# Conv 2's difference plane in three rounded passes in a fused residual block of two 3x3 convolutions

## The reference

```python
def _conv3x3(x, w): ...                     # NCHW, stride 1, padding 1
def _bn(x, gamma, beta, mean, var):
    inv = gamma * rsqrt(var + EPS)
    return x * inv[None, :, None, None] + (beta - mean * inv)[None, :, None, None]
identity = x
out = relu(_bn(_conv3x3(x, w1), g1, b1, m1, v1))
out = _bn(_conv3x3(out, w2), g2, b2, m2, v2)
return relu(out + identity)
```

## Time and profile before

| | |
|---|---|
| median of 3 runs | 596.51 us (595.66 to 597.7) |
| the profiled execution | 596.25 us |
| its span, first to last instruction | 594.3 us |
| PE busy | 576.5 us, 97% of the span |
| PEld busy | 533.7 us, 90% |
| DVE busy | 555.3 us, 93% |
| ACT busy | 472.6 us, 80% |
| mean granted TensorE clock | 0.994 |

### The profile page before, as it was taken

One profiled execution on the slowest core, in us unless ns is written; L12 is line 12 of the kernel. 1 busy time (PEld: TensorE's weight loads), 2 busy tenths in 40 slices (PEclk: granted clock), 3 DMA queues, 4 the chain that ended last, 5 costly groups with the idle time before them and its releaser, 6 DMA issues.

```text
span 594.3 us, 8667 instructions
## 1 busy us (share of the span) xinstructions
PE 576.5 (97%) x2962; PEld 533.7 (90%) x2962; DVE 555.3 (93%) x475; ACT 472.6 (80%) x730; POOL 19.8 (3%) x28
## 2 busy tenths in 40 slices
PE   6769999999999999999999999999999999999997
PEld 3769999999999999999999999999999999999996
DVE  6899999999999999999999999999999999999963
ACT  5687888887788887788887778888778888778874
POOL 7500000000000000000000000000000000000000
PEclk9799999999999999999999999999999999999999
DMA  4112223322223331232332222332122233121012
GB/s 161 56 61 88 104 84 110 112 82 82 83 83 110 110 108 56 83 109 84 110 110 67 89 92 83 110 110 93 71 83 93 100 110 110 58 82 51 29 55 108
DMA packets 22458, 53.23 MB, mean 90 GB/s; under 512 B 1584, under 2 KB 18096, under 8 KB 22448
## 3 DMA queue, kind: packets, MB, share of 16 engines
q1 hardware_dynamic: 22304, 52.80, 25.0%
q10 hardware_dynamic: 144, 0.29, 0.2%
HBM read 27.40 MB, written 25.69 MB: 89 GB/s over the span
## 4 chain that ended last, share of the span: by engine, by line
PE 93%; DVE 2%; ACT 1%; issue 0%; POOL 0%
PE psum L639 93%; DVE x_outer L367 1%; DVE x_lo L375 1%; DVE psum L389 1%; ACT w_mat L488 0%; DVE t_outer L412 0%; POOL g_t L181 0%; ACT psum L514 0%; DVE t_inner L398 0%; DVE x_inner L355 0%; ACT out_sb L563 0%; ACT z L534 0%; ACT z L535 0%; DVE x_inner L359 0%
## 5 line engine op out<-in xcount | busy, mean ns | idle before, releaser
L639 PE MATMUL psum<-x_hi,w_hi 128*128 128x392 f32 (+2 forms) x512 | 175.3, 342 | 6.7 <-DVE x_lo L375 6.7
L639 PE MATMUL psum<-x_hi,w_lo 128*128 128x392 f32 (+2 forms) x512 | 175.8, 343 | 0.0
L639 PE MATMUL psum<-x_lo,w_hi 128*128 128x392 f32 (+2 forms) x512 | 175.1, 342 | 0.0
L389 DVE TENSOR_TENSOR psum<-psum,z 128x784 f32<-128x784 f32 (+1 forms) x128 | 127.1, 993 | 21.3 <-ACT hidden L540 9.9
L639 PEld LDWEIGHTS psum<-x_hi,w_hi 128*128 128x128 f32 x512 | 97.0, 189 | 8.3 <-issue 4.8
L639 PEld LDWEIGHTS psum<-x_hi,w_lo 128*128 128x128 f32 x512 | 97.0, 189 | 0.4
L639 PE MATMUL psum<-t_inner,w_mat 128*128 128x392 f32 x256 | 94.7, 492 | 2.7 <-ACT psum L514 2.7
L639 PEld LDWEIGHTS psum<-x_lo,w_hi 128*128 128x128 f32 x512 | 97.0, 189 | 0.4
L563 ACT ACTIVATE out_sb<-psum 128x784 f32<-128x784 f32 x64 | 52.8, 825 | 47.1 <-PE psum L639 47.0
L639 PE MATMUL psum<-h_lo,w_hi 128*128 128x392 f32 x256 | 87.3, 341 | 0.0
L639 PE MATMUL psum<-h_hi,w_hi 128*128 128x392 f32 x256 | 87.2, 341 | 0.0
(11 more groups left out here) (67 smaller groups left out, 747.5 us busy)
## 6 DMA issues: line engine op xcount, KB each, us to landing
x_sb<-x_dram SPq DMA_DIRECT2D x32, 814.0 KB, 4.3
out_dram<-out_sb SPq DMA_DIRECT2D x64, 392.0 KB, 2.8
w_raw<-w_dram ACTq DMA_DIRECT2D x1, 288.0 KB, 3.5
w_raw<-w_dram SPq DMA_DIRECT2D x1, 288.0 KB, 5.4
bn<-params_dram SPq DMA_DIRECT2D x1, 132.0 KB, 3.7
```

Source lines behind the costliest of these rows:

```text
L389: nc.vector.tensor_tensor(psum[:, half, EVEN:ODD + 1, 0:width], t1, z[:, half, :, 0:width], ALU.add).then_inc(joined[conv], 1)
L639: ins = nc.tensor.matmul(psum[:, half, bank, first:first + (j1 - j0) * WQ], w[:, i, far, :], moving, start=not onto and at == 0, stop=at = ...
```

## The change

- T2 of conv 2 is treated as T1 is: `high_hidden("inner")` on ACT and `split_hidden("inner")` on DVE take both inner planes of `t_inner` in one instruction each (`ti_hi`, `ti_lo`), and its product is three rounded passes.
- The semaphore that releases ACT's rounding is now raised by `difference_hidden`, not by `sum_hidden`. PE waits for `hlo_ready["inner"]` ahead of both inner products. `sum_hidden` no longer waits for PE, since PE no longer reads `t_inner`.
- `x_inner` and `x_outer` have rows of 29 instead of 28 columns; `outer_x` subtracts one run of 812 elements a plane.
- `x_hi` and `x_lo` lose their zero edge rows, and POOL the eight memsets; conv 1's products skip the edge in their indices.
- `w_raw`, `g_t` and `g_sum` lie in the tiles `z` (conv 1) and `out_sb` (conv 2).
- The loop covers steps 2 to 25; 26 to 33 are written out. The first load of image 1 is written ahead of the steps.
- In the tail's step N both inner planes are split together, half by half.

The core of the diff:

```diff
+    RUN = NQ * (WQ + 1)
-        x_outer = sb("x_outer", [P, 2, NQ, WQ])
-        x_inner = sb("x_inner", [P, TBUFS, 2, NQ, WQ])
+        x_outer = sb("x_outer", [P, 2, RUN])
+        x_inner = sb("x_inner", [P, TBUFS, 2, RUN])
-        t1_hi = sb("t1_hi", [P, NP, WQ], F32R)
-        t1_lo = sb("t1_lo", [P, NP, WQ], F32R)
+        ti_hi = sb("ti_hi", [P, 2, NP, WQ], F32R)
+        ti_lo = sb("ti_lo", [P, 2, NP, WQ], F32R)
+        spare = {1: z[:].rearrange("p h s r -> p (h s r)"), 2: out_sb[:].rearrange("p h s r -> p (h s r)")}
-            with eng.Fori(0, (N - 4) // 4) as turn:
+            with eng.Fori(0, (N - 8) // 4) as turn:
-            for s in range(N - 2, N + 2):
+            for s in range(N - 6, N + 2):
-            if which == "t1":
-                return t_inner[:, 0, rows], t1_hi[:, rows], t1_lo[:, rows]
+            if which == "inner":
+                return t_inner[:, :, rows], ti_hi[:, :, rows], ti_lo[:, :, rows]
-            for t in (x_hi, x_lo):
-                for b in range(2):
-                    for row in (0, NQ + 1):
-                        nc.gpsimd.memset(t[:, b, :, row, :].bitcast(F32), 0.0).then_inc(zeroed, 1)
...
-                nc.vector.tensor_tensor(x_outer[:], cells[:, :, :, 0:WQ], cells[:, :, :, 1:WQ + 1],
+                nc.vector.tensor_tensor(x_outer[:], runs(cells, 0, XPLANE), runs(cells, 1, XPLANE),
                                         ALU.subtract).then_inc(tx_ready["outer"], 1)
...
-                wait(dve, inner[2], 4 * n)
+                wait(dve, hlo_ready["inner"], n)
                 nc.vector.tensor_tensor(t_inner[:, 0, rows], hid_data[:, 0, rows, 0:WQ], hid_data[:, 1, rows, 0:WQ],
-                                        ALU.add).then_inc(th_ready["t1"], 1)
+                                        ALU.add)
...
-                                        ALU.subtract).then_inc(th_ready["t2"], 1)
+                                        ALU.subtract).then_inc(th_ready["inner"], 1)
...
                 if last:
-                    split_hidden("t1", s - 1, kl % 2)
+                    split_hidden("inner", s - 1, kl % 2)
...
                 if last:
-                    high_hidden("t1", s - 1, kl % 2)
+                    high_hidden("inner", s - 1, kl % 2)
...
-                if (conv, i) == (2, 2):
-                    return ((t_inner[:, 1], wmat[2]),)
-                elif i == 1:
-                    hi, lo = t1_hi, t1_lo
+                elif i in (1, 2):
+                    hi, lo = ti_hi[:, i - 1], ti_lo[:, i - 1]
...
-                pe.wait_ge(th_ready["t2"], n + 1 + more)
+                pe.wait_ge(hlo_ready["inner"], n + 1 + more)
                 pe.wait_ge(res_ready, 2 * n + half + 1)
                 sum_products(2, half, 2, SUM_T2, passes_of(2, 2, 0), True).then_inc(inner[2], 1)
-
-                pe.wait_ge(hlo_ready["t1"], n + 1 + more)
                 sum_products(2, half, 1, SUM_T1, passes_of(2, 1, 0), True).then_inc(inner[2], 1)
```

More of the change, by code:

```diff
@@ L31, in residual_block @@
     WQ = W // 2
-    assert P == 128 and N % 4 == 0
+    assert P == 128 and N % 4 == 0 and N > 8
     HALF1 = ((0, (NP + 1) // 2), ((NP + 1) // 2, NP))
@@ L65, in residual_block, with scratch @@
         out_sb = sb("out_sb", [P, 2, 2, (NQ // 2) * WQ])
-        w_raw = {1: sb("w1_raw", [P, 3, 3, C]), 2: sb("w2_raw", [P, 3, 3, C])}
+        spare = {1: z[:].rearrange("p h s r -> p (h s r)"), 2: out_sb[:].rearrange("p h s r -> p (h s r)")}
+        def scratch(conv, at, kinds):
+            size = kinds * 3 * C
+            return spare[conv][:, at:at + size].rearrange("p (k h c) -> p k h c", k=kinds, h=3)
+        w_raw = {conv: scratch(conv, 0, 3) for conv in (1, 2)}
         bn = sb("bn", [P, 8 + 4 * C])
@@ L75, in residual_block @@
         bias = sb("bias", [P, 2])
-        g_t = {1: sb("g1_t", [P, 4, 3, C]), 2: sb("g2_t", [P, 4, 3, C])}
-        g_sum = {1: sb("g1_sum", [P, 3, C]), 2: sb("g2_sum", [P, 3, C])}
+        g_t = {conv: scratch(conv, 9 * C, 4) for conv in (1, 2)}
+        g_sum = {conv: scratch(conv, 21 * C, 1)[:, 0] for conv in (1, 2)}
         wmat = {1: sb("w1_mat", [P, 4, 2, P]), 2: sb("w2_mat", [P, 4, 2, P])}
@@ L111, in residual_block @@
         xlo_ready = {"inner": sem("xlo_inner"), "outer": sem("xlo_outer")}
-        th_ready = {"t1": sem("th_t1"), "t2": sem("th_t2"), "outer": sem("th_outer")}
-        hhi_ready = {"t1": sem("hhi_t1"), "outer": sem("hhi_outer")}
-        hlo_ready = {"t1": sem("hlo_t1"), "outer": sem("hlo_outer")}
+        th_ready = {"inner": sem("th_inner"), "outer": sem("th_outer")}
+        hhi_ready = {"inner": sem("hhi_inner"), "outer": sem("hhi_outer")}
+        hlo_ready = {"inner": sem("hlo_inner"), "outer": sem("hlo_outer")}
         inner = {1: sem("inner1"), 2: sem("inner2")}
@@ L230, in newton_step, with runs, until @@
             after(eng.tensor_tensor(inv[:, part], inv[:, part], tmp[:, part], ALU.mult))
[L232 to L238, removed]
+        def runs(cells, first, step):
+            return cells[:, first:first + 2 * step].rearrange("p (s r) -> p s r", s=2)[:, :, 0:RUN]
         def x_full(which, k):
             full, places = (x_outer[:], slice(0, 2)) if which == "outer" else (x_inner[:, k], slice(2, 4))
-            return full.rearrange("p s j q -> p s (j q)"), places
+            return full.rearrange("p s (j c) -> p s j c", c=WQ + 1)[:, :, :, 0:WQ], places
         def x_part(t, k, places):
-            return t[:, k % 2, places, 1:NQ + 1, :].rearrange("p s j q -> p s (j q)")
+            return t[:, k % 2, places]
+        def until(n, k):
+            return (n - k % 2) * 8 + 16
         def hidden_rows(half):
@@ L277, in _ @@
             load(sp, 0, 0)
[L278 removed]
+            sp.dma_start(w_raw[2], w2).then_inc(w_in[2], 16)
+            load(sp, 1, 1)
             def step(s, k):
[L281 removed]
+                if not isinstance(s, int) or 0 <= s < N - 2:
                     wait(sp, tx_ready["outer"], s + 3 - XBUFS)
@@ L513, in residual @@
                 for i, bank, share in ((0, SUM_T1, 0.5), (1, SUM_T2, -0.5)):
-                    ins = nc.scalar.activation(psum[:, half, bank, 0:width],
-                                               x_inner[:, k, i, j0:j1, :].rearrange("p j q -> p (j q)"),
-                                               ACT.Copy, scale=share)
+                    ins = nc.scalar.activation(psum[:, half, bank, 0:width].rearrange("p (j q) -> p j q", q=WQ),
+                                               x_full("inner", k)[0][:, i, j0:j1], ACT.Copy, scale=share)
                 ins.then_inc(res_ready, 1)
@@ L522, in high_hidden @@
                 act.wait_ge(th_ready[which], n + 1 + (half or 0))
-                wait(act, *((inner[2], 4 * n) if which == "t1" else (outer[2], 2 * (n - 1))))
+                wait(act, *((inner[2], 4 * n) if which == "inner" else (outer[2], 2 * (n - 1))))
                 nc.scalar.activation(hi, full, ACT.Copy).then_inc(hhi_ready[which], 1)
@@ L571, in step @@
                     residual(N - 1, kl, 0)
-                    high_hidden("t1", N - 1, kl % 2, 0)
+                    high_hidden("inner", N - 1, kl % 2, 0)
                     relu_hidden(N - 1, 1)
@@ L576, in step @@
                     copy_sum(2, N - 1, 0)
-                    high_hidden("t1", N - 1, kl % 2, 1)
+                    high_hidden("inner", N - 1, kl % 2, 1)
                     residual(N - 1, kl, 1)
```

35 lines of the change are left out of this document (21 added, 14 removed).

## The result

The changed kernel takes 639.25 us, median of 4 runs (637.29 to 640.38), against 596.09 us (595.57 to 597.7) for the kernel before: ratio 1.0716, interval 1.0681 to 1.075. The forecast was 639.7 us, 631 to 648.

The account below looks back on a forecast made before the run. PE's list bound the kernel at 17.62 us a period; a closed round of waits would replace it at 19.06. 29 x (19.06 - 17.62) = 41.8, + 1.2 + 0.5 = 43.5 on 596.25: 639.7 us, range 631 to 648.

Parts of the forecast that it names:

- J: DVE's join that begins a period; the walk starts from it at 0 and reaches the next one at 19.06 us.
- HH: ACT's rounding of the inner planes; waits for difference_hidden, starts at 2.92 us, grows from 0.89 to 1.55 us.
- RO: ACT's relu_out, queued behind the rounding; starts at 4.38 us and ends at 5.21.
- K: DVE's join that waits for relu_out; starts at 5.34 us instead of 4.48, DVE standing still for 0.86 us.
- TI: DVE's split of both inner planes; starts at 7.17 us, ends at 9.01, lengthened by 0.85 us.
- E: PE's first inner product of a period; its first matmul waits for the whole split and starts at 9.07 us.
- the detour over RO: DVE's join waits for relu_out, queued behind ACT's rounding: 0.86 us a period; without it the round is 18.20 us.
- A: Rival: PE keeps the bound and its 15.4 us saving is kept, 580.9 us; chance 0.05.
- B: Rival: the waits hide and DVE's list alone decides, 17.90 us a period, 606.0 us; chance 0.03.
- C: Rival: only the split's length counts, relu_out coming early enough, 18.20 us a period, 614.8 us; chance 0.04.
- rival D: The main case with TensorE's clock falling in each pause, 2.85 us lost each time, 723 us; chance 0.03.
- The end: Last full step +0.57 us, tail's two inner products save 0.48, 0.4 given back for its split waits: +0.5 us.

Follow-up runs that it names:

- RO ahead of the rounding: The changed kernel with ScalarE's relu_out of conv 2's half 0 put ahead of the rounding of the two inner planes: 614.81 us.
- the split ahead of sum_x as well: The changed kernel with relu_out ahead of the rounding and, on VectorE, the split of the two inner planes ahead of sum_x: 601.66 us.
- half the split: The changed kernel with VectorE splitting only the sum plane; the difference plane's third pass reads the sum plane's low part: 613.45 us.
- three passes for half 1 only: The kernel before with the difference plane in three rounded passes for half 1 of the rows, relu_out ahead of the rounding: 588.96 us.
- three passes for half 0 only: The kernel before with three rounded passes for half 0 and the plain product for half 1, halves exchanged against the mixed kernel: 608.78 us.
- the first two experiments: The changed kernel with relu_out ahead of the rounding, 614.81 us; then with the split ahead of sum_x as well, 601.66 us.

## Why the prediction was right

**The bound and its replacement** held. The walk had, from J at 0: HH at 2.92, RO at 4.38, K at 5.34, TI at 7.17, E at 9.07, next J at 19.06. The rows of after give 303.52 - 300.60 = 2.92, 4.39, 5.30, 7.13, 9.03 and 19.04. The experiments then priced the terms one by one. The means over the 29 periods from J of step 2 to J of step 31 are:

| kernel | J of step 2, us | J of step 31, us | mean period, us |
|---|---|---|---|
| before | 49.41 | 560.37 | 17.62 |
| after | 53.30 | 604.68 | 19.01 |
| RO ahead of the rounding | 51.72 | 579.41 | 18.20 |
| the split ahead of sum_x as well | 51.16 | 566.61 | 17.77 |
| the three passes undone | 52.48 | 617.98 | 19.50 |
| half the split | 49.41 | 576.70 | 18.18 |
| three passes for half 1 only | 48.47 | 552.22 | 17.37 |
| three passes for half 0 only | 49.63 | 572.93 | 18.04 |

So the detour over RO costs 0.81 us a period (walked: 0.86), TI's added length 0.83 (0.85), the passes on PE give 0.49 (0.48), and DVE's list alone stands at 17.77 (17.90).

**The rivals.** A (PE keeps the bound) falls with the rows of after and with the plain product put back, which cost 14 us although PE had 1.62 us to spare. The Trainium skill (Perfetto Trace Analysis, Identifying the Most-Contended Engine) has the engine with the highest occupancy optimized first, and judges TensorE's headroom by MFU and its weight loads, not by its busy matmuls. By the weight loads the trace does not single out PE, as the prediction had it: the weight loads were busy 477.38 of 510.96 us, and DVE 492.84. That PE was the bound follows from its having no pause, and the measurement shows that relieving it does not pay where the new handoff closes a longer round and DVE gets the work. B and C were real as limits lying under the round: the first two experiments uncovered them in turn, C at 18.20 us and B at 17.77.

**The mis-sized terms** were the steady part, the start and the end. They cancelled in part, and that 639.25 us lies within 0.5 us of the forecast is partly luck. The steady part gave 551.38 - 510.96 = 40.4 us (forecast 41.8), from a period of 19.01 instead of 19.06. The start gave 53.30 - 49.41 = 3.9 us in the first profiles, where 1.2 was forecast, and 50.25 - 48.66 = 1.6 in the second ones, whose times differ by 41.9 us. In the first profile of the changed kernel E itself began where it was expected:

```profile
40.66 0.66 PE L650 MATMUL psum<-ti_hi,w_hi 128*128 128x392 f32 x1 [2.83 <-DVE ti_lo L430]
```

at 40.66 against the forecast 40.63. From there to J took 12.64 us instead of the steady 19.04 - 9.03 = 10.01, at a granted clock of 0.50 (1.2 GHz) for the first part:

```profile
42.00:44.00 2.00, 2.00 (x7) 2.00 (x7) 2.00 (x2) 1.01 (x3) 0.00 (x0) 0.50 0.03 8
```

In its second profile the same pause of 2.83 us was followed by a granted clock of 1.00 (2.4 GHz), with 13 matmuls instead of 7 in the same stretch, and from E to J it took 50.25 - 40.35 = 9.90 us:

```profile
40.35 0.42 PE L650 MATMUL psum<-ti_hi,w_hi 128*128 128x392 f32 x1 [2.83 <-DVE ti_lo L430]
```

```profile
42.00:44.00 2.00, 2.00 (x13) 1.98 (x12) 2.00 (x3) 2.00 (x5) 0.00 (x0) 1.00 0.00 0
```

So the 2.7 us between them are the clock's. That is rival D in one step out of thirty, and the one sign of being wrong named by the prediction, the granted clock leaving 1.00, that came true. The step of the prediction that failed is the argument against D, "the clock in that stretch stayed at 1.00" after pauses of 2.63 and 2.73 us: it was read from one execution, and in others the clock fell after such pauses. For the 1.6 us pauses of the steady stretch its conclusion stood, at 1.00 over 551 us. The end was forecast at +0.5 and gave nothing, 30.63 instead of 30.68 us from J of step 31 to the end of ACT's last `relu_out` (635.31 - 604.68 and 591.05 - 560.37): the 0.4 us that I gave back for waits of the tail's own splits did not arise. PE waits for the last time in step 31,

```profile
612.76 0.45 PE L650 MATMUL psum<-ti_hi,w_hi 128*128 128x392 f32 x1 [0.70 <-DVE ti_lo L430]
```

and runs without a pause from there.

The two idle times were forecast too long, PE's at 1.92 us (1.62 in the mean, 1.61 in the period shown) and K's at 0.86 (0.73), while the period held. The walk counted from start to start, and a pause in the profile begins only when the last record before it ends: the matmul at 307.68 would be followed 0.18 later, at 307.86, which is 1.77 us ahead of E, and E's own first matmul is followed 0.28 later instead of 0.18. Together that is 1.87 us, the difference between 19.01 and PE's 17.14.

## What to carry to other kernels

Where more than one engine runs at 90% or more, walk the round before counting work: from one instruction over every handoff back to the same instruction one period later. If that is longer than the fullest engine's list, it sets the period, and every microsecond on it is paid, idle engines or not. Here work taken from the bound engine paid only where what it needs instead was ready ahead of the place that needs it: the same three passes cost 13 us on the first of two products and gave 7 on the second.

## What was not expected

TensorE's granted clock in the first full step differs between executions of the same kernel. Each of the ten further profiles, that of the kernel before included, has a pause of 2.33 to 2.70 us at about 31 us, and the clock was at 0.50 for some us soon after it. At E a second pause followed. After 1.95 to 2.88 us of it the clock fell again in four profiles; it stayed at 1.00 after 1.99 us (half the split), 2.46 (three passes for half 0) and 2.83 (the changed kernel's second profile). In the one trace on which the prediction rests it fell after neither pause, 2.63 nor 2.73 us. So the length of the pause alone does not decide it; what does stays open. The pauses of 0.4 to 1.64 us that some kernels have in every period never lowered it. J of step 2 in the changed kernel came at 53.30 us in one execution and at 50.25 in the other, so a start that was measured once is good to about 3 us.
